# A graph layer on one core: gather program written out, one-hot columns and second norm in PSUM

## What is computed

```
xn = layernorm(x)
summed = segment_sum(xn[src], dst); counts = segment_sum(1, dst)
gnn = relu((summed / max(counts, 1)) @ W_l.T + b_l + xn @ W_r.T) + xn
Q = elu(xn @ Wq) + 1;  K = elu(xn @ Wk) + 1;  v = xn @ Wv
msg = attention(Q, sum K v, sum K) @ Wm;  msg = layernorm(msg, g1, b1)
h = relu(concat(xn, msg) @ W1) @ W2
mix = xn + layernorm(h, g2, b2)
x = x + gnn + mix
out = x + feed_forward(layernorm(x))  # for the rows with the largest router weights
```

## Time and profile before

| | us |
|---|---|
| median of 3 runs | 3382.6 (3373.04 to 3392.79) |
| span of the profiled execution, first to last instruction | 2897.3 |
| the profiled execution's own time | not given beside its span |
| of the span: from the first gather call to the end of the last | 2096.7 |
| of the span: behind the last gather | 666.5 |
| POOL busy | 1710.6 |
| TensorE (PE) busy | 2227.7 |
| VectorE (DVE) busy | 1485.6 |
| ScalarE (ACT) busy | 953.9 |

### The profile page before, as it was taken

The page is one execution under the profiler, slowest core; times in us unless marked ns, Lnnn a source line. Parts: engine busy times, 40 slices in busy tenths (PEclk is TensorE's granted clock), DMA queues, the critical chain, the costliest instruction groups (busy, mean ns, idle before and its releaser), DMA issues.

```text
span 2897.3 us, 51918 instructions
## 1 busy us (share of the span) xinstructions
PE 2227.7 (77%) x13208; PEld 1895.8 (65%) x13209; DVE 1485.6 (51%) x3876; ACT 953.9 (33%) x2179; POOL 1710.6 (59%) x1782
## 2 busy tenths in 40 slices
PE   0188888887877778778877887778877899149998
PEld 0076677765766666666666766666666778139998
DVE  7644445443443444444444444444544688774444
ACT  4733333321222222212222222122222799115554
POOL 3177777777777777777777777777776000013332
PEclk7599999997888898888888889889989999569999
DMA  6765555554444444444444444444443799102221
GB/s 215 243 178 176 172 168 177 174 167 143 132 131 126 135 128 134 126 135 128 133 127 136 126 133 129 134 128 127 133 133 95 234 312 308 66 26 66 65 65 45
DMA packets 230281, 413.69 MB, mean 143 GB/s; under 512 B 38273, under 2 KB 129795, under 8 KB 230126
## 3 DMA queue, kind: packets, MB, share of 16 engines
q0 software_dynamic: 81536, 224.87, 27.3%
q1 hardware_dynamic: 143454, 183.57, 19.3%
q10 hardware_dynamic: 5136, 3.81, 0.4%
HBM read 315.79 MB, written 96.32 MB: 142 GB/s over the span
## 4 chain that ended last, share of the span: by engine, by line
POOL 33%; PE 24%; issue 21%; DVE 12%; DMA 5%; DVEq 3%; ACT 1%; POOLq 1%; SPq 0%; ACTq 0%
POOL gath_raw L586 33%; PE ps L1488 10%; PE ps L1362 6%; DMA gath_raw<-xtab,stage 4%; PE ps L1293 3%; PE ps L1295 2%; DVEq L391 2%; DVE work L878 1%; DVE work L875 1%; DVE stats L672 1%; DVE work L862 1%; DVE agg L914 1%; DVE stats L779 1%; DVE agg L721 1%; DVE gath_raw L644 1%
## 5 line engine op out<-in xcount | busy, mean ns | idle before, releaser
L586 POOL DMA_INDIRECT gath_raw<-xtab,stage x1568 | 1558.9, 994 | 522.0 <-issue 454.5
L1293 PE MATMUL ps<-gath_raw,onehot 128*128 128x256 f16 x1952 | 517.6, 298 | 397.1 <-DMA gath_raw<-xtab,stage 293.3
L713 DVE SCALAR_TENSOR_TENSOR onehot<-iota,blkbase,dstF 128x512 f16 x488 | 365.8, 750 | 475.8 <-issue 310.5
L1293 PEld LDWEIGHTS ps<-gath_raw,onehot 128*128 x1952 | 204.4, 105 | 512.4 <-issue 475.4
L1295 PE MATMUL ps<-gath_raw,onehot 128*128 128x257 f16 x1952 | 520.6, 299 | 0.0
L721 DVE TENSOR_TENSOR agg<-agg,ps x488 | 204.5, 419 | 445.4 <-PE ps L1295 440.5
L1362 PE MATMUL ps<-work,w_s 128*128 128x256 f32 x1568 | 403.8, 417 | 0.0
L1362 PEld LDWEIGHTS ps<-work,w_s 128*128 128x128 f32 x1568 | 329.6, 216 | 53.4
L1488 PE MATMUL ps<-split_raw 128*128 128x256 f32 x2376 | 293.0, 285 | 1.7 <-DVE split_raw L992 1.5
L1488 PEld LDWEIGHTS ps<-split_raw 128*128 128x128 f32 x2376 | 288.1, 193 | 2.4 <-issue 1.9
L1134 ACT ACTIVATE small<-small 128x2 f32<-128x2 f32 x98 | 19.9, 203 | 680.9 <-DVE small L787 680.9
(11 more groups left out here) (184 smaller groups left out, 3148.2 us busy)
## 6 DMA issues: line engine op xcount, KB each, us to landing
work<-x_in SPq DMA_DIRECT2D x98, 256.0 KB, 3.6
gath_raw<-xtab,stage POOLq DMA_INDIRECT x1568
ff_d<-work SPq DMA_DIRECT2D x49, 512.0 KB, 3.4
work<-x_in SPq DMA_DIRECT2D x14, 896.0 KB, 7.3
xtab<-gath_raw SPq DMA_DIRECT2D x14, 896.0 KB, 4.9
xt_d<-work SPq DMA_DIRECT2D x49, 256.0 KB, 4.3
q_d<-work SPq DMA_DIRECT2D x49, 256.0 KB, 2.3
work<-q_d SPq DMA_DIRECT2D x49, 256.0 KB, 3.5
```

What stands on the lines that cost most here:

```text
L586: e.indirect_dma_start(out=gath[:, TPG * s + t, 0:2 * D], out_offset=None, in_=xtab[:, :], in_offset=bass.IndirectOffsetOnAxis(ap=stage[:, ...
L713: v.scalar_tensor_tensor(out=onehots[:, ds(p % 2 * TPG, TPG), :], in0=iota16[:, :].unsqueeze(1).to_broadcast(shape), scalar=blkbase[:, ds( ...
L1293: t.matmul(ps[:, ds(BG + p % 2, 1), 0:D], oh, gath[:, k, 0:D], start=q == 0, stop=False, skip_group_check=True)
```

## The change

- The gather program on POOL is written out for all 392 groups. Each call takes its indices straight from `srcI`; `stage`, its copies and its semaphore are gone. The waits for `grp_used` ask for the same groups as before.
- `iota16` is gone. VectorE copies the single-precision `iotaf` once into columns 384 to 511 of banks BG and BG+1, and each one-hot reads it there, from the bank whose turn it is.
- `mn2` is gone. ScalarE writes the second norm back into bank BF, in place; VectorE multiplies and adds in place, and the last addition reads it from there. Therefore the next product into BF waits for `m_r` in place of `m_n2`, and ScalarE's wait for `m_r` is gone.

```diff
-            def gather(i, h, n):
-
-                c = srcI[:, ds(RING * i, n), :] if not isinstance(i, int) else srcI[:, RING * i:RING * i + n, :]
-                e.tensor_copy(stage[:, h, 0:n, :], c).then_inc(stage_set, 1)
-                e.wait_ge(stage_set, i + 1)
-                alone(e, stood)
-                for s in range(n):
-                    if past(i, 1):
-                        e.wait_ge(grp_used, RING * (i - 1) + s + 1)
-                        alone(e, stood)
-                    for t in range(TPG):
-                        e.indirect_dma_start(
-                            out=gath[:, TPG * s + t, 0:2 * D], out_offset=None, in_=xtab[:, :],
-                            in_offset=bass.IndirectOffsetOnAxis(ap=stage[:, h, s, t:t + 1], axis=0)
-                        ).then_inc(rows_in[s], 16)
-            steps(e, lambda i, h, j: gather(i, h, RING), NG // RING, 2)
-            gather(NG // RING, NG // RING % 2, NG % RING)
+            for g in range(NG):
+                s = g % RING
+                if g >= RING:
+                    e.wait_ge(grp_used, g - RING + 1)
+                    alone(e, stood)
+                for t in range(TPG):
+                    e.indirect_dma_start(
+                        out=gath[:, TPG * s + t, 0:2 * D], out_offset=None, in_=xtab[:, :],
+                        in_offset=bass.IndirectOffsetOnAxis(ap=srcI[:, g, t:t + 1], axis=0)
+                    ).then_inc(rows_in[s], 16)
...
+            for k in range(2):
+                v.tensor_copy(ps[:, BG + k, IOTA_AT:IOTA_AT + P], iotaf[:, :]).then_inc(iota_ps, 1)
+            e.wait_ge(iota_ps, 2)
...
-                                       in0=iota16[:, :].unsqueeze(1).to_broadcast(shape),
+                                       in0=ps[:, ds(BG + p % 2, 1), IOTA_AT:IOTA_AT + P].to_broadcast(shape),
...
-                own.link(v.tensor_tensor(mn2, mn2, bcast(g2_s[:, :], 2), ALU.mult))
-                own.link(v.tensor_tensor(mn2, mn2, bcast(b2_s[:, :], 2), ALU.add))
+                h2 = bank(BF)
+                own.link(v.tensor_tensor(h2, h2, bcast(g2_s[:, :], 2), ALU.mult))
+                own.link(v.tensor_tensor(h2, h2, bcast(b2_s[:, :], 2), ALU.add))
                 e.wait_ge(m_xs, i + 1)
-                v.tensor_tensor(mr[s], mn2, mr[s], ALU.add).then_inc(m_r, 1)
+                v.tensor_tensor(mr[s], h2, mr[s], ALU.add).then_inc(m_r, 1)
...
             def m_norm2(i, base):
                 e.wait_ge(m_v2, i + 1)
-                if past(i, 1):
-                    e.wait_ge(m_r, i)
-                m_normed(mn2, bank(BF), 1, base, m_n2)
+                m_normed(bank(BF), bank(BF), 1, base, m_n2)
...
             def m_mlp_out(i):
                 e.wait_ge(m_h1, 2 * i + 2)
                 if past(i, 1):
-                    e.wait_ge(m_n2, i)
+                    e.wait_ge(m_r, i)
```

More of the change, by code:

```diff
@@ L169, in build @@
         headm = sb("headm", [P, P])
-        iota16 = sb("iota16", [P, P], f16)
         iotaf = sb("iotaf", [P, P])
@@ L175, in build @@
         onehot = sb("onehot", [P, 2, TPG, P], f16)
-        stage = sb("stage", [P, 2, RING, TPG], i32)
         bnd = sb("bnd", [1, 2 * NG], i32)
@@ L200, in build @@
         BA, BB, BC, BD, BE, BF, BG = range(7)
+        IOTA_AT = 384
         G_T = (BA, BD)
@@ L238, in build @@
         ones_set = sem("ones_set")
-        stage_set = sem("stage_set")
+        iota_ps = sem("iota_ps")
         k_x_in = [sem(f"k_x_in{i}") for i in range(3)]
@@ L338, in build @@
         mh1 = part(work, 4608, (4, SB))
-        mn2 = part(work, 6656, (2, D))
         mr = [part(work, 5632 + 512 * s, (2, D)) for s in range(2)]
@@ L557, in _ @@
                             base=LASTROWS, pattern=[[0, 1]], channel_multiplier=-1).then_inc(cst, 1)
-            e.iota(iota16[:, :], pattern=[[1, P]], base=0, channel_multiplier=0,
-                   allow_small_or_imprecise_dtypes=True).then_inc(cst, 1)
             e.iota(iotaf[:, :], pattern=[[1, P]], base=0, channel_multiplier=0,
@@ L698, in _ @@
             v.memset(vaug[:, :, :, P:P + 1], 1.0).then_inc(k_ones, 1)
-            e.wait_ge(cst, 11)
+            e.wait_ge(cst, 10)
             e.wait_ge(agg_zero, NBLK // 14)
```

## The result

The change takes 3456.4 us (median of 4 runs, 3449.5 to 3458.5), the kernel before 3385.8 in the same set. The ratio is 1.019, with a 95% interval of 1.016 to 1.022. Forecast were 3250 us.

A forecast was written before the change was run, and what follows sets the result against it. POOL's issuing of 1568 gather calls was taken as the bound. Gains of 60 and 75 us less 3 us for the cover make 132: 3382.6 - 132 = 3250.6, said as 3250 us; range for 8 in 10 3220 to 3300.

The forecast's parts named there:

- I hold this remainder constant, which no row can show: Outside the profiled span: the 485.3 us by which the median 3382.6 exceeds it were taken as unchanged.
- POOL sets the pace: Gather stage: lasts as long as POOL takes to issue 1568 calls, 2097 us; TensorE, VectorE and ScalarE fit in between.
- Part A: POOL's staging copies of indices, every six groups: removing them gains 60 us, all on the path.
- Part B: Gather calls on POOL lengthened by VectorE instructions with two SBUF inputs: PSUM inputs remove this, gaining 75 us.
- the port: SBUF access: a VectorE instruction with two SBUF inputs holds up a gather call, which ends 0.82 us after it.
- One-hot and norm steps at no price: VectorE: 488 one-hots and three norm steps with PSUM input cost 0; at best 0.06 us gained per one-hot.
- The moved wait of the second MLP product: TensorE's line 1372 now waits for VectorE's residual add of the iteration before, which ends long before: 0.
- the cover: TensorE's idle time in the gather stage suffices for a faster POOL, thinly near the end; 3 us taken off.
- The sum: Whole kernel: 60 + 75 - 3 = 132 us gained.
- 25 us of new waits: New TensorE waits that set the upper end, 3270, of the forecast's own range.
- the fetching of straight code: POOL's written-out program must be fetched, running slower than before, for instance 3439 us; chance 0.02, and 0.02 for eating just the gain.
- TensorE becomes the bound: Gather stage: half of the long-call gain lost to new waits, 3288 us, POOL waiting for the ring; chance 0.09.

The follow-up runs named there:

- the gather part alone: Kernel before with only the gather program written out and indices taken straight from srcI; one-hot and second norm stay in SBUF: 1.0026 and 1.0009 (late).
- the paused change: The change plus a small memset and a wait for it on POOL behind each group of four calls: 3345.2 and 3349.9 us (late), 3049.7 us (prompt).

## Why the prediction was wrong, and what in it was right

- **The step that failed** is the sentence "I hold this remainder constant, which no row can show". The median stood 485 us above the span, and I took it for time around the span. It was time inside it: in every later execution, late or prompt, only 1.7 to 2.0 us lie around the span, and the late kernel before has 480 us more in its gather stage. The trace and the times were of two conditions. All terms of the sum were read from the prompt one and applied to a median of the late one, where POOL isn't the bound.
- **What bounds the kernel**, "POOL sets the pace": right in the trace, wrong in the timed runs. There POOL waits 555 us for the ring, for VectorE's additions, and these wait 650 us for TensorE's completions, with a median lag of 3.7 us.
- **Part A**, 60 us: nothing in the late condition (1.001 and 1.003). In the prompt one it wasn't run alone; the whole is 133.4 us and its PSUM parts 73.7, which leaves 59.7.
- **Part B**, 75 us, by the port: measured 59.3 and 14.4 in the prompt condition. In the late one the calls are as short (946 ns), and the time rises by 1.3% where it should have fallen by 2.2%.
- **One-hot and norm steps at no price**: the one-hot is 748 ns against 750 in the earlier trace rows; the 0.69 named as the best case didn't come. Right as a zero.
- **The moved wait of the second MLP product and the cover**: right in the prompt condition, where POOL never waits for the ring.
- **The sum** of 132 us: 133.4 measured, where the trace was valid. Two side sums of the prediction don't come out: 132 and 17 are 149, not 152 (0.095 us a call), and 25 us of new waits on 3250 are 3275, above the 3270 given. Neither touches the forecast.
- **The rivals**: the slower side was given to the fetching of straight code. That was the wrong mechanism, since the written-out program alone is 0.9996. "TensorE becomes the bound" had the right place, and the sign that I named for it, waits of POOL for the ring, is what the profile shows. But TensorE isn't the bound: it is busy for 69% of the stage after the change, against 81% in the earlier trace rows, and its completions are late.

What is shown of the loss: it occurs only where completions are late, most of it comes with the PSUM part, and a pause on POOL more than removes it. What is argued: that without long calls POOL's run is more even and so delays completions more. The median lags fit in part (3.7 us in the kernel before, 3.75 with the gather part alone, 4.9 to 5.1 with the one-hot in PSUM, 4.4 to 5.1 in the change), but the paused change has 4.2, more than the kernel before, and is faster than it. And no run separated even calls from the reading of PSUM, nor either of them from the lower clock of the stage. Open too: why TensorE's completions are late in one condition and not in the other, and what decides which is met. The traces of the late condition have fewer records of semaphore updates (19183 after the change, 42879 in the first trace), which may be why the views say "remote"; whether that is a cause or only goes with it, no run tells.

## What to carry to other kernels

Compare the span of a trace with the time of the runs first. Where they differ by more than a few us, the trace isn't of these runs, and no sum from it can be set against their median; profile the timed state anew before pricing anything. And where "remote" waits stand on a single core, measure the lag from producer to consumer: if completions are late, a change that frees the issuing engine can make the kernel slower and a pause on it faster, as both did here, so a change has to be timed in both conditions (the change is 0.954 in one and 1.016 to 1.019 in the other; with the pause it is 1.052 and 0.985 to 0.989).

## What the runs showed of the hardware that I had not expected

- The same program on one core takes 2899 or 3385 us from set to set, on chip 2 the one and the other, each within 0.8% of its median. Of the 491 us between the two profiles 480 lie in the stage in which POOL issues 1568 indirect DMAs (2577 us long, against 2097).
- In the longer one TensorE's completions reach VectorE with a median lag of 3.7 us and up to 23 us, in the shorter with 0.3 us. VectorE's own reach TensorE in 0.31 us in both.
- In the longer one 0.97 us between groups of four calls, in place of 0.30, gain 98 us, and half the bytes change nothing. Most additions with a long lag begin 1 to 3 us after POOL's last call, but 63 of 137 products with such a lag outlived a pause of 0.97 us.
- A gather call that starts inside a VectorE instruction with two SBUF inputs ends 0.82 us after it. Taking one input from PSUM removes that: in the changed kernel (prompt) the mean of a call is its median, 946 ns, and one call of 1568 is longer than 0.97 us.
